# Another order of work, first transfers and weight split in the first steps of a three-layer CIN kernel

## What is computed

```python
for i, S in enumerate([128, 128, 128]):
    Fk = h.shape[1]                        # 39, 64, 64
    Wr = Ws[i].reshape(39, Fk, S)
    out = relu(einsum('bfd,bgd,fgs->bsd', x, h, Wr) + bs[i][None, :, None])
    if i != 2:
        h, direct = out[:, :64], out[:, 64:]
    else:
        direct = out
    outs.append(direct)
result = sum(concatenate(outs, axis=1), axis=-1)
```

## Time and profile before

| | |
|---|---|
| median of 3 runs | 589.99 us (589.92 to 590.31) |
| the profiled execution | 589.6 us, of which the span is 587.8 us |
| PE busy | 559.3 us (95%) |
| DVE busy | 535.4 us (91%) |
| POOL busy | 517.4 us (88%) |
| ACT busy | 375.5 us (64%) |
| TensorE clock granted, mean | 0.985 |

### The profile page before, as it was taken

How to read it: one execution, slowest core, us unless ns; L and a number is a source line. 1 busy time by engine, 2 the same in 40 slices (tenths; PEclk the granted TensorE clock), 3 DMA queues, 4 the chain that set the end, 5 groups by cost and what they waited for, 6 DMA issues and landing times.

```text
span 587.8 us, 7877 instructions
## 1 busy us (share of the span) xinstructions
PE 559.3 (95%) x2032; PEld 384.8 (65%) x2032; DVE 535.4 (91%) x514; ACT 375.5 (64%) x421; POOL 517.4 (88%) x231
## 2 busy tenths in 40 slices
PE   1795999999999999999999999999999999999997
PEld 0363666676767667676766767676676767667765
DVE  3665989999999999999999999999999999999975
ACT  2555567585766758576675857667585766758663
POOL 1593997989899898989989898998989899898995
PEclk9797999999999999999999999999999999999999
DMA  8997651845749285574818557392855738163001
GB/s 309 420 418 281 227 214 64 302 183 167 300 129 339 72 295 200 166 298 131 341 66 295 202 166 298 126 342 70 294 204 167 297 134 336 68 212 106 0 3 36
DMA packets 26787, 121.61 MB, mean 207 GB/s; under 512 B 3242, under 2 KB 3370, under 8 KB 24468
## 3 DMA queue, kind: packets, MB, share of 16 engines
q1 hardware_dynamic: 26772, 121.44, 57.1%
HBM read 120.90 MB, written 0.52 MB: 207 GB/s over the span
## 4 chain that ended last, share of the span: by engine, by line
PE 87%; POOL 5%; issue 4%; DMA 1%; DVE 1%; ACT 1%; SPq 0%; POOLq 0%; ACTq 0%
PE acc L451 87%; POOL z_lo L223 5%; DMA xfirst<-x 1%; DVE z_raw L334 0%; ACT h L521 0%; ACT last L521 0%; DVE z_whole L334 0%; ACT z_hi L518 0%; DVE z_hi L221 0%; DVE sums L357 0%; ACT xrep_psum L538 0%; DVE z_lo L220 0%; SPq L252 0%; SPq L253 0%; POOLq L212 0%
## 5 line engine op out<-in xcount | busy, mean ns | idle before, releaser
L223 POOL TENSOR_TENSOR z_lo<-z_raw,z_hi 128x1024 fp32r<-128x1024 f32 (+2 forms) x224 | 511.6, 2323 | 53.9 <-ACT z_hi L518 53.9
L518 ACT CAST z_hi<-z_raw 128x1024 fp32r<-128x1024 f32 (+2 forms) x224 | 224.9, 1017 | 115.6 <-DVE z_raw L334 84.2
L334 DVE TENSOR_TENSOR z_raw<-h,xwide 128x1024 f32<-128x1024 f32 x192 | 229.9, 1218 | 19.8 <-ACT h L521 16.4
L451 PE MATMUL acc<-z_hi,w_hi 128*128 128x512 f32 (+2 forms) x560 | 222.9, 467 | 7.8 <-ACT z_hi L518 7.1
L451 PE MATMUL acc<-z_hi,w_lo 128*128 128x512 f32 (+2 forms) x560 | 183.4, 397 | 0.0
L451 PE MATMUL acc<-z_lo,w_hi 128*128 128x512 f32 (+1 forms) x528 | 171.9, 399 | 5.6 <-DVE z_hi L221 3.3
L451 PEld LDWEIGHTS acc<-z_hi,w_hi 128*128 128x128 f32 (+2 forms) x560 | 106.2, 190 | 69.6 <-issue 50.1
L451 PEld LDWEIGHTS acc<-z_hi,w_lo 128*128 128x128 f32 (+2 forms) x560 | 105.9, 189 | 28.6 <-issue 3.8
L451 PE MATMUL acc<-z_whole,w_whole 128*128 128x512 f32 x256 | 122.3, 601 | 0.0
L451 PEld LDWEIGHTS acc<-z_lo,w_hi 128*128 128x128 f32 (+1 forms) x528 | 99.0, 189 | 33.0 <-POOL z_lo L223 5.3
L334 DVE TENSOR_TENSOR z_psum<-h,xwide 128x1024 f32<-128x1024 f32 x64 | 78.3, 1224 | 0.1
(11 more groups left out here) (16 smaller groups left out, 90.8 us busy)
## 6 DMA issues: line engine op xcount, KB each, us to landing
xwide<-x SPq DMA_DIRECT2D x160, 512.0 KB, 4.7
xfirst<-x SPq DMA_DIRECT2D x15, 2048.0 KB, 7.8
xwide<-w SPq DMA_DIRECT2D x2, 1024.0 KB, 13.4
xfirst<-x SPq DMA_DIRECT2D x1, 1280.0 KB, 8.1
xfirst<-x SPq DMA_DIRECT2D x1, 768.0 KB, 9.6
w_whole<-w_rest SPq DMA_DIRECT2D x1, 512.0 KB, 11.5
w<-w0a SPq DMA_DIRECT2D x1, 409.5 KB
direct<-w0b SPq DMA_DIRECT2D x1, 409.5 KB
```

Source lines behind the costliest of these rows:

```text
L223: return eng.tensor_tensor(lo[0:rows, 0:n, :], z[0:rows, 0:n, :], hi[0:rows, 0:n, :].bitcast(F32), ALU.subtract)
L334: nc.vector.tensor_tensor(dst, in0, in1, ALU.mult).then_inc(made[kind], 1)
L451: return nc.tensor.matmul(dst, w[0:rows, PLACE[layer, t], :], z[0:rows, t - G * g, :], start=first and t == 0, stop=final and t == TILES[l ...
L518: nc.scalar.copy(z_hi[0:rows, slot("PV", pair, par, pos, HI_RING), 0:n, :], src).then_inc(hi_made, 1)
```

## The change

- Step 0 gets an order of its own; without layer 2 it is 1 1 1 1 0 0 0 0 1 1 1 1 1 1. Step 1's order has one more layer 1 group ahead of layer 2.
- The first transfer brings three slots of xfirst instead of five, and stands ahead of w0a and w0b, which now have 128 rows. Bias is moved behind the unsplit weights; xfirst of block 1 is issued after four groups of x instead of six, w2 after six as before.
- Layer 2's w_lo is made by DVE at the end of step 0 instead of by POOL ahead of (1,6).
- The subtraction of step 0's last V group is done in step 0.
- DVE first writes a tile of zeros. PE runs 16 matmuls on it before step -1 and 8 between steps -1 and 0, into acc[2].

```diff
+SCHEDULE_0 = "111100001111112222222222"
-SCHEDULE_1 = "112222222111000011111222"
+SCHEDULE_1 = "111222222211000011111222"
...
-        w0 = sb("w0", [P0, T0, SIZE])
+        w0 = sb("w0", [128, T0, SIZE])
+        zeros = sb("zeros", [128, N], F32R)
...
+            load_first(0, xfirst_head_in, range(0, 1 + G))
             sp.dma_start(w0[:], w0a).then_inc(w0_in, 16)
             sp.dma_start(w0t, w0b).then_inc(w0_in, 16)
-            load_first(0, xfirst_head_in, range(0, 1 + 2 * G))
-            load_first(0, xfirst_in, range(1 + 2 * G, 1 + T0))
+            load_first(0, xfirst_in, range(1 + G, 1 + T0))
+            sp.dma_start(stage[1][:, 0:SPLIT_COUNT[1], :], w1).then_inc(w_staged[1], 16)
+            load_wide(0, 0, 0)
+            sp.dma_start(w_whole[:], w_rest).then_inc(w_whole_in, 16)
             sp.dma_start(bias[:], b).then_inc(bias_in, 16)
-            sp.dma_start(stage[1][:, 0:SPLIT_COUNT[1], :], w1).then_inc(w_staged[1], 16)
-            for g in range(ASIDE):
+            for g in range(1, 4):
                 load_wide(0, 0, g)
-                if g == 0:
-                    sp.dma_start(w_whole[:], w_rest).then_inc(w_whole_in, 16)
             sp.wait_ge(*made_all(-1, 0))
             load_first(1, xfirst_in)
+            for g in range(4, 6):
+                load_wide(0, 0, g)
             sp.dma_start(stage[2][:, 0:SPLIT_COUNT[2], :], w2).then_inc(w_staged[2], 16)
...
             sp.wait_ge(w1_lo_made, 1)
-            sp.wait_ge(w_lo_made, len(SPLIT0) + 1)
+            sp.wait_ge(w2_lo_made, 1)
...
-                    elif g == (2 if first else 0):
+                    elif g == (1 if first else 0):
                         dve.wait_ge(xfirst_in, 16 * (j + 2))
...
-                for p in late[:-1] if order(j)[-1][2] == "V" else late:
+                kept = order(j)[-1][2] == "V" and not (isinstance(j, int) and j == 0)
+                for p in late[:-1] if kept else late:
                     subtract(*p[1:])
...
+            zero = z_whole[:, WHOLE_RING - 1, 0, :]
+            nc.vector.memset(zero, 0.0).then_inc(zero_set, 1)
+            dve.wait_ge(zero_set, 1)
+            nc.vector.tensor_copy(zeros[:], zero).then_inc(zeros_made, 1)
...
-            a, n = SPLIT_FROM[1], SPLIT_COUNT[1]
-            dve.wait_ge(w_hi_made, len(SPLIT0) + 1)
-            nc.vector.tensor_tensor(w_lo[:, a:a + n, :], stage[1][:, 0:n, :], w_hi[:, a:a + n, :].bitcast(F32),
-                                    ALU.subtract).then_inc(w1_lo_made, 1)
+            split(1).then_inc(w1_lo_made, 1)
             step(-1, 1)
+            split(2).then_inc(w2_lo_made, 1)
...
-                    if (layer, g) == SPLIT2_BEFORE and isinstance(j, int) and j == 0:
-                        split(stage[2][:, 0:SPLIT_COUNT[2], :], SPLIT_FROM[2], SPLIT_COUNT[2], 128, len(SPLIT0) + 2)
                     if kind == "P":
                         subtract(pair, par, pos)
...
                     if layer == 2 and isinstance(j, int) and j == 1:
-                        pe.wait_ge(w_lo_made, len(SPLIT0) + 1)
+                        pe.wait_ge(w2_lo_made, 1)
...
+            def keep_clock(n):
+                for _ in range(n):
+                    nc.tensor.matmul(acc[2][:, :], zeros[:, 0:SIZE], zeros[:], start=True, stop=True)
+            pe.wait_ge(zeros_made, 1)
+            keep_clock(WARM_START)
             pe.wait_ge(w0_folded, 1)
             step(-1, 0)
+            keep_clock(WARM_H0)
             pe.wait_ge(w_whole_in, 16)
```

More of the change, by code:

```diff
@@ L67 @@
 STEP = steps(SCHEDULE)
-STEP_1 = steps(SCHEDULE_1)
+BEGIN = [steps(SCHEDULE_0), steps(SCHEDULE_1)]
 def order(j):
     if isinstance(j, int):
-        return [e for e in (STEP_1 if j == 1 else STEP) if 0 <= j + (1, 0, -1)[e[0]] < BLOCKS]
+        return [e for e in (BEGIN[j] if 0 <= j < len(BEGIN) else STEP) if 0 <= j + (1, 0, -1)[e[0]] < BLOCKS]
     return STEP
@@ L120 @@
 SPLIT2_BEFORE = (1, 6)
-ASIDE = 6
+WARM_START, WARM_H0 = 16, 8
 assert len(SPLIT0) > 0 and SPLIT_COUNT[1] <= 16 and SPLIT_COUNT[2] <= 16
@@ L161, in cin @@
                  xwide[:, 1, T12 - 8:T12 - 4, :].rearrange("p a (b s) -> p (a b) s", s=SIZE)]
-        w0t = direct[:].rearrange("p a (b s) -> p (a b) s", s=SIZE)[0:P0, 0:T0, :]
+        w0t = direct[:].rearrange("p a (b s) -> p (a b) s", s=SIZE)[:, 0:T0, :]
         w0_in = sem("w0_in")
@@ L170, in cin @@
         w1_lo_made = sem("w1_lo_made")
+        w2_lo_made = sem("w2_lo_made")
+        zero_set = sem("zero_set")
+        zeros_made = sem("zeros_made")
         bias_in = sem("bias_in")
@@ L250, in refill @@
                         load_wide(j + 1, par, g)
+            load_first(0, xfirst_head_in, range(0, 1 + G))
             sp.dma_start(w0[:], w0a).then_inc(w0_in, 16)
             sp.dma_start(w0t, w0b).then_inc(w0_in, 16)
-            load_first(0, xfirst_head_in, range(0, 1 + 2 * G))
-            load_first(0, xfirst_in, range(1 + 2 * G, 1 + T0))
+            load_first(0, xfirst_in, range(1 + G, 1 + T0))
+            sp.dma_start(stage[1][:, 0:SPLIT_COUNT[1], :], w1).then_inc(w_staged[1], 16)
+            load_wide(0, 0, 0)
+            sp.dma_start(w_whole[:], w_rest).then_inc(w_whole_in, 16)
             sp.dma_start(bias[:], b).then_inc(bias_in, 16)
-            sp.dma_start(stage[1][:, 0:SPLIT_COUNT[1], :], w1).then_inc(w_staged[1], 16)
-            for g in range(ASIDE):
+            for g in range(1, 4):
                 load_wide(0, 0, g)
-                if g == 0:
-                    sp.dma_start(w_whole[:], w_rest).then_inc(w_whole_in, 16)
             sp.wait_ge(*made_all(-1, 0))
             load_first(1, xfirst_in)
+            for g in range(4, 6):
+                load_wide(0, 0, g)
             sp.dma_start(stage[2][:, 0:SPLIT_COUNT[2], :], w2).then_inc(w_staged[2], 16)
-            for g in range(ASIDE, G12):
+            for g in range(6, G12):
                 load_wide(0, 0, g)
-            for g in range(ASIDE):
+            for g in range(G12 - 4):
                 load_wide(1, 1, g)
@@ L272, in _ @@
             sp.wait_ge(w1_lo_made, 1)
-            sp.wait_ge(w_lo_made, len(SPLIT0) + 1)
-            for g in range(ASIDE, G12):
+            sp.wait_ge(w2_lo_made, 1)
+            for g in range(G12 - 4, G12):
                 load_wide(1, 1, g)
@@ L364, in step @@
                 late = []
-                if (not isinstance(j, int) or j > 0) and order(j - 1)[-1][2] == "V":
+                if (not isinstance(j, int) or j > 1) and order(j - 1)[-1][2] == "V":
                     late.append((V_LAG - 1, pair + par - 1, 1 - par, len(order(j - 1)) - 1))
@@ L376, in step, with split @@
                         late.append((pos + V_LAG, pair, par, pos))
-                for p in late[:-1] if order(j)[-1][2] == "V" else late:
+                kept = order(j)[-1][2] == "V" and not (isinstance(j, int) and j == 0)
+                for p in late[:-1] if kept else late:
                     subtract(*p[1:])
+            def split(layer):
+                a, n = SPLIT_FROM[layer], SPLIT_COUNT[layer]
+                dve.wait_ge(w_hi_made, len(SPLIT0) + layer)
+                return nc.vector.tensor_tensor(w_lo[:, a:a + n, :], stage[layer][:, 0:n, :],
+                                               w_hi[:, a:a + n, :].bitcast(F32), ALU.subtract)
+            zero = z_whole[:, WHOLE_RING - 1, 0, :]
+            nc.vector.memset(zero, 0.0).then_inc(zero_set, 1)
+            dve.wait_ge(zero_set, 1)
+            nc.vector.tensor_copy(zeros[:], zero).then_inc(zeros_made, 1)
             dve.wait_ge(w0_in, 32)
@@ L426, in _ @@
             for i, (a, ts) in enumerate(SPLIT0):
-                split(w0[:, ts[0]:ts[-1] + 1, :], a, len(ts), P0, i + 1)
+                split(w0[0:P0, ts[0]:ts[-1] + 1, :], a, len(ts), P0, i + 1)
             for par in range(2):
@@ L599, in _ @@
             for a, ts in SPLIT0:
-                split(w0[:, ts[0]:ts[-1] + 1, :], a, len(ts), P0)
+                split(w0[0:P0, ts[0]:ts[-1] + 1, :], a, len(ts), P0)
             for pos, (_, _, kind) in enumerate(order(-1)):
@@ L624 @@
     w0 = np.asarray(L0_rec_W0).reshape(FIELDS, FIELDS, SIZE)
-    w0a = np.zeros((PER, FIELDS, T0, SIZE), np.float32)
-    w0b = np.zeros((PER, FIELDS, T0, SIZE), np.float32)
+    w0a = np.zeros((128, T0, SIZE), np.float32)
+    w0b = np.zeros((128, T0, SIZE), np.float32)
     f = np.arange(FIELDS)
@@ L630 @@
         g = (f + s) % FIELDS
-        w0a[s // T0, :, s % T0] = w0[f, g]
+        rows = FIELDS * (s // T0) + f
+        w0a[rows, s % T0] = w0[f, g]
         if s:
-            w0b[s // T0, :, s % T0] = w0[g, f]
+            w0b[rows, s % T0] = w0[g, f]
     pairs = [(t, T12 + t if t < T12 - 1 else t) for t in range(T12)]
@@ L660 @@
         "x0": x0,
-        "w0a": w0a.reshape(P0, T0, SIZE),
-        "w0b": w0b.reshape(P0, T0, SIZE),
+        "w0a": w0a,
+        "w0b": w0b,
         "w1": some(w1, 1, False),
```

## The result

The changed kernel takes 585.53 us in the median (583.86 to 586.10, 4 runs), the kernel before 589.95 (588.79 to 590.31, 4 runs). The ratio is 0.9926, with a 95% interval of 0.9906 to 0.9947. So it is faster by 4.4 us (0.7%), where 7.7 were forecast, and 0.3 us outside the stated range. The profiled execution took 586.1 us, the longest of the four, its span 584.3.

What follows compares the result with a forecast made beforehand. PE's own work bounds the loop, and all lost time lies ahead of 62 us. Profiled 589.6 less 7.7 (step 0's earlier end, nothing for step 1) is 581.9, plus 0.4 for the median 582.3; range 580.5 to 585.2.

Steps and rivals of the forecast that it cites:

- What bounds the kernel: In the loop PE's own work is the limit, 31.00 of 31.00 us; all lost time lies ahead of 62 us.
- Step -1: First transfers and zero matmuls: PE's first real matmul at 10.8, (0,1) at 11.4, relu0 at 19.5 instead of 19.69.
- The zero matmuls cost nothing while they fit in pauses: Around step -1: 16 zero matmuls end by 9.3, before 10.8; 8 take 1.9 to 3.8 us in a 3.87 us pause.
- Step 0: Walk in the new order: PE ends the step at 44.7 instead of 52.44 and resumes at 47.85 instead of 55.59.
- R - S: Time from PE's first real matmul of step 0 to that of step 1; the prediction's walk had 24.65 us.
- PE's decides, 44.7: End of step 0: of PE's limit, 44.7, and POOL's, 44.3, PE's sets the end.
- Rival 1: Clock stays low or falls again in steps -1 and 0; price 2.0 to 2.5 us, 584.5 in total; chance 0.20.
- Step 1, "I count nothing here": Behind PE's restart: waits for z_lo hide the low clock; 0 counted, ends 0.9 us of gain and 1.0 of loss.
- the sum's 581.9: Whole kernel: profiled execution of 589.6 less 7.7 us of gain.
- Weight split and subtraction: End of step 0 on DVE: split 2.69 us, to 44.3, hidden with 1.2 to spare; subtraction through at 41.6.
- Rival 3: DVE's weight split gets between POOL's (1,7) and (1,8) in step 0; (1,8) waits 2.3 us, total 584.5; chance 0.06.
- Rivals 2, 4 and 5: Block 1's xfirst no earlier, 584.8 (0.05); step 0 all at 1.2 GHz, 601.9 (0.02); loop returns the gain, 589.8 (0.03).

Runs made afterwards that it cites:

- e3: Changed kernel with 14 instead of 8 zero matmuls before step 0 and more in the pauses of steps 0 and 1; 581.83 us.
- e8: e3 with step -1 filled too: 22 instead of 16 zero matmuls ahead of it, 5 and 4 in group (0,1); 581.62 us.
- e1: Changed kernel without its 24 zero matmuls (DVE still writes the zeros); 583.55 us.
- e14: e1 again, on the chip of e13; 583.51 us.
- e13: The changed kernel itself, run again beside e14 on one chip; 585.66 us.
- e2: Changed kernel with 14 instead of 8 zero matmuls between steps -1 and 0 and 5 more in step 0's first group; 584.30 us.
- e15: e8 with step 1's old order (P W, then layer 2); 581.37 us.
- e5: e3 with layer 2's weight split back on POOL, ahead of (1,6); 586.78 us.
- e6: e3 with step 0's last V subtraction put off as before the change; 584.71 us.
- e9: e8 with the old order of the first transfers: w0 ahead of five slots, xfirst of block 1 behind six x groups; 584.88 us.
- e12: e8 with step 1's relu1 behind z_hi of (1,0), layer 2's split behind (1,0)'s product, and no 12 zero matmuls ahead of step 1; 580.70 us.
- e16: e12 with layer 2's weight split on DVE two products later, behind (1,2) instead of (1,0); 579.61 us.
- e10: Changed kernel with only the 16 zero matmuls at the start, none between steps -1 and 0; 585.01 us.
- e7: e3 with the old order of step 0 (layer 0 between the last groups of layer 1); 583.07 us.

## Why the prediction missed

The step that failed is the clock in the walks of steps 0 and 1: the forecast takes PE's own sum at 2.4 GHz (44.7) and puts the low clock behind the restart at nothing. The profiled execution ran 6.8 us of each step at 1.2 GHz and lost 3.1 and 1.6 us by it. With the clock held (e3, e8) the kernel takes 581.8 and 581.6 us, within 0.7 us of the forecast 582.3. Without any zero matmuls it takes 583.9 (e1, e14), so by the means about half of the 3.2 us missing are falls that come anyway, and half come with the change's own zeros.

- *What bounds the kernel*: right. All of the gain lies ahead of 62 us; the loop is unchanged.
- *Step -1*: the transfers did better than the bounds (fold at 7.78 instead of 8.4, PE's first matmul at 10.28; (0,1)'s product began at 10.90, where 11.2 was the early end). relu0 came at 18.94 against 19.5, outside its 19.2 to 20.0. That everything hangs on the transfer for (0,1) held: DVE waited 0.77 us for it, and PE 0.78 for the z_lo made from it.
- *"The zero matmuls cost nothing while they fit in pauses"*: wrong. They fit, and still the kernel is about 1.6 us slower with them (e1, e13, e14), at least in part because they move the clock's fall. The prediction priced them as time on PE, not by what they do to the clock.
- *Step 0*: the walk was right for the clock it assumed, R - S 24.8 in e2, e3, e8 and e15 against 24.65. The assumption failed. "PE's decides, 44.7" was the sentence that should have decided the forecast: once PE is the limit of a step, time lost at 1.2 GHz comes through, and the earlier trace rows had such a stretch in this very place. The stretch at 0.50 made R - S 27.7, a shorter one in e13 made it 26.2.
- *Rival 1* was this, and had 0.20. It deserved most of the chance. Its argument against, that the zeros fill half of the pause, did not hold: a half-filled pause only put the fall off. In size it gave 584.5; what it left out is the next line.
- *Step 1, "I count nothing here"*: this is the term that was mis-sized, 0 with 1.0 of loss as its end, where 1.6 were measured. I argued that the waits for z_lo hide the low clock. They do in the kernel before (528.5, where e3 with a held clock has 528.6), but not in the changed kernel, 530.1, where the clock rose at 58.6 instead of 60.3 but PE had resumed 5.1 us earlier, so the low stretch reached 8.2 us behind the restart instead of 4.8. In the profiled execution 3.1 us in step 0, less 0.5 from the transfers, and 1.6 behind the restart make 4.2: its 586.1 against the sum's 581.9. e13's profiled execution adds up the same way: 1.5 and 0.8 less 0.3 make 2.0, its 583.93 against 581.9. The median of the four executions, 585.53, misses 582.3 by 3.2; of the unprofiled ones only the fastest, 583.86, shows a higher mean clock (0.990 against 0.985).
- *Weight split and subtraction*: the split was hidden, as forecast, in e8 (ended 44.30, relu1 ended 45.83). Its place is worth about 4.0 us (e5), near POOL's 4.60 in the earlier trace rows. What the subtraction's place is worth by itself is open, since e6's 2.1 us are in the main the held POOL group.
- *Rival 3* did not come in the changed kernel, but e6 shows its mechanism and its size, 2.1 us where 2.3 were estimated.
- *Rivals 2, 4 and 5* fell: copy_xrep came at 24.89, step 0 was not slow throughout, and the loop gave nothing back.

## What to carry to other kernels

Where PE is the limit of a stretch, work out the forecast at both of TensorE's clock levels and read from the granted clock what the engine did before it fell; the time in between is run-to-run spread. Here it grew with the tighter schedule: all executions of the kernel before lie between 588.56 and 591.05, those of the changed one between 583.51 and 587.78. In this kernel zero matmuls in all pauses of the start-up kept the clock (worth 2 us over none, and the spread fell to 0.1 us), and zeros in only some of them were worse than none. A standstill is worth a look at what stands in front on the releasing engine, and at every wait of the engine that stands: of PE's 3.15 us 1.0 was an order on ACT, and the other 2.1 the read of an accumulator that PE is about to overwrite. When two paths are late at once, a difference such as R - S can hide one of them (e9). And a run's median can move because its executions fall on the other side of a clock's fall, so compare executions at equal clock (e12, e16).

## What the runs showed of the hardware

- The clock does not fall while matmuls on zeros fill PE's pauses: in e8, with 67 of them, the granted clock stays at 2.4 GHz from 6.8 us to the end, and its four executions lie within 0.1 us; e15 with the same zeros has it from 5.4 us on.
- The clock fell around short waits too, not only in a standstill of 3 us: at 16.3 us in e2 and at 16.0 in e10, 0.6 and 0.3 us after PE had stood 1.2 us for z_lo. The same step -1 kept its clock through that place in other executions (changed kernel, e13).
- The low stretch differs between executions of one kernel: in step 0 the clock was at 0.5 from 24.5 to 31.3 in the changed kernel's profile and from 24.8 to 28.2 in e13's.
- DVE's subtraction of 128x2048 out of SBUF takes 2.28 us when it starts before POOL's (e12), and 2.50 to 3.58 when it starts while POOL's is under way (e7, e8, e16, e6). POOL's group takes 3.25 (e12) and 4.43 us (e6) instead of 2.35 to 2.4 when it comes second. In e6, where both came second once, each ended 2.15 to 2.23 us behind the end of the one before it, so nearly its own full length.
